# Attention and fp8 feed-forward kernel: the values' products of every head group split over two places, fixed PSUM banks for the side jobs, and four vector and GpSimd steps moved

## The chip, the cores and the metric

The kernel runs on one core of a Trainium2 chip. The metric is the device time of one execution in microseconds (us). Shown are the median of three timed runs and one execution taken by the hardware profiler. The engines are named as in the profile: PE is TensorE, with PEld its weight loads, DVE is VectorE, ACT is ScalarE, POOL is GpSimd, and SP is SyncE, which here issues nearly all DMAs.

## The reference, cut to what matters

Input x has 16 batch rows of 512 tokens with 256 features; there are 16 heads of 16.

```
xn   = layernorm(x)
qkv  = xn @ w_qkv.T + b_qkv
att  = softmax(causal(q k^T / 4 + position_bias))      # position_bias from cos/sin tables and a constant
attn = (att @ v) @ w_proj.T + b_proj
ffn  = bf16(fp8(xn / s_in) @ fp8(kernel / s_k) * s_in * s_k) + bias
out  = x + attn + ffn
```

## The kernel before

The program handles one batch row `b` at a time. The rows 1 to 13 are iterations of one loop; rows 0, 14 and 15 are written out. Every engine has its own instruction stream, and semaphores order them.

**Groups, slots and chunks.** A row has four head groups `g` of four heads. TensorE goes through 12 slots `k` per group, so a row is 48 places (g, k). In each slot it makes one bank of transposed scores (keys by queries, for row b and group g, banks `scoreT_a`, `scoreT_b`, `scoreT_c` in turn; line 648, and 651 for the position features of groups 0 and 1) and, two groups ahead, one bank of scores the other way round (`score_a` to `score_c`, line 625). ScalarE turns the first kind into exponentials in `probs` (L1013); VectorE takes row maxima from the second (L1101, "chunk"). Slots 0 to 3 are 512 columns wide, slots 4 to 7 have 384, and slots 8 to 11 hold 256 and 128. With three banks of each kind TensorE can be three slots ahead of ScalarE and VectorE, no more.

**Side jobs.** After the scores of a slot TensorE runs the jobs that the tables at the head of the file put there. They are:

- `PV`: probabilities times values of the group before (L674), 8 matmul rows per key tile j = 0 to 3. It needs `mask` of POOL for its tile. In some groups the first key tile is made at `PV_AT` and the rest at `PV_REST_AT`.
- `MT`: the transposed row maxima of the next group (L610, L611). It waits for `max_hi` of ScalarE (L908, after the exponential of slot 1), and ScalarE then writes `neg_max_T` (L914), which SP sends into the stacks.
- `QK` and `V` (L560): products of the row after, read by ScalarE (`qk_parts`, `v_rows`) and, for QK, by VectorE (L1089).
- `FF`: the feed-forward product in bf16 (L603), read by ScalarE into `Y1` (L1036; it shares memory with `xnT_bf`).
- `PJ`: the projection of the row before (L560), read by VectorE in `result` (L1114), which stands behind the chunk of slot 1 in group 3.
- `T`: transposes of the normalised input of the row after the next (L568).

All side jobs write to two PSUM banks, `misc_a` and `misc_b`. Each job waits until the reader of the job before it in the same bank is done (function `misc`, table `done`). The kernel before gives the banks in turn along the order of the jobs.

**The other engines around the change.** VectorE also takes statistics for the row after the next (`stats`, L1068), inverts the softmax denominators (`invert`, L1108), and makes three steps of the fp8 quantiser, `quant_magic` (L1125 of 1024 elements, then two of L1130 with two inputs from SBUF). POOL masks (L1324), quantises, computes 1/std (`rstd`, L1291 to L1297), multiplies the attention output by the inverse denominators (`divide`, L1358), splits it (`attn_parts`, L1363), and adds the biases and the feed-forward result. ScalarE rounds the divided attention in `attn_hi` (L992), which `attn_parts` waits for. SP stores the inverses to a scratch tensor in HBM and spreads them back (`store_recips` L411, `spread_recips` L423) into the memory of `XN`, from which `divide` reads.

A job at (g, k) is done by all engines at their own place (g, k); the tables with `_AT` hold these places.

## Time and profile before

| | us |
|---|---|
| median of three runs | 767.23 (766.87 to 767.3) |
| the profiled execution | 769.2 |
| its span, first to last instruction | 767.2 |

The span is 2.0 us short of the profiled execution's time, and close to the median of the others. Granted TensorE clock over the span: 0.99.

| engine | busy, us | share of the span |
|---|---|---|
| PE | 738.7 | 96% |
| DVE | 634.6 | 83% |
| ACT | 586.1 | 76% |
| POOL | 532.4 | 69% |

The end of a matmul is modelled, so the PE share says little on how closely TensorE is packed. What counts is at which time the next instruction starts and what released it. The iterations of the loop are alike within a few hundredths of a microsecond, so one of them stands for all; the rows below are from the iteration of row 6, which covers the time from about 309 to 354 us. In times such as "(2,0)" the first number is the group and the second the slot.

### The profile page before, as it was taken

Reading aid. Unit: us, or ns where it says so; the run is one execution under the profiler, and the core shown is the slowest. Engines: PE = TensorE matmul, PEld = TensorE weight load, DVE = VectorE, ACT = ScalarE, POOL = GpSimd, SP = SyncE. Lnnn points to the kernel's source line nnn. Section 1 sums busy time; section 2 is a strip of 40 time slices with the busy share of each in tenths; the row PEclk is TensorE's granted clock in tenths of the full one; section 3 lists DMA queues with packets and bytes.
Section 4 is the critical chain, followed back from the end, with each engine's and each line's share of the span. In section 5 each row is a group of like instructions: output and inputs, shape, how many; then the busy total and the mean of one; then the engine's idle time right before and its main releaser. Section 6 shows DMA issues by size and latency. Waiting matters only on the chain.

```text
span 767.2 us, 23128 instructions
## 1 busy us (share of the span) xinstructions
PE 738.7 (96%) x6285; PEld 475.1 (62%) x6285; DVE 634.6 (83%) x2401; ACT 586.1 (76%) x1263; POOL 532.4 (69%) x525
## 2 busy tenths in 40 slices
PE   7989999999999999999999999999999999999987
PEld 4656556666765666566566656666665666666555
DVE  4898798889989888988988898898988889888613
ACT  4557888787888878788887878878787888877662
POOL 7445767786777778776777868677776867767571
PEclk9999999999999999999999999999999999999889
DMA  5442353435335433533544253244425334443201
GB/s 181 150 152 103 128 176 142 139 118 178 117 138 174 153 127 118 184 128 121 174 153 141 112 187 136 108 170 152 158 95 193 133 120 153 160 148 108 88 32 62
DMA packets 55313, 105.65 MB, mean 138 GB/s; under 512 B 10421, under 2 KB 30389, under 8 KB 55285
## 3 DMA queue, kind: packets, MB, share of 16 engines
q1 hardware_dynamic: 53968, 104.52, 38.3%
q10 hardware_dynamic: 1316, 0.80, 0.4%
q8 instruction: 13, 0.21, 0.1%
q14 instruction: 16, 0.12, 0.1%
HBM read 18.42 MB, written 8.90 MB: 36 GB/s over the span
## 4 chain that ended last, share of the span: by engine, by line
PE 68%; ACT 11%; DVE 8%; issue 6%; DMA 2%; SPq 2%; DVEq 1%; ACTq 1%; POOLq 0%; POOL 0%
PE misc_a L560 13%; PE misc_a L674 10%; PE misc_b L560 9%; PE scoreT_b L648 9%; PE scoreT_a L648 5%; PE score_c L625 4%; PE misc_b L674 3%; ACT probs L1013 3%; PE score_a L625 2%; PE scoreT_b L651 2%; ACT qk_parts L901 2%; ACT attn_hi L992 2%; DVE row_max L1101 2%; SPq L351 1%; ACT out_T L986 1%
## 5 line engine op out<-in xcount | busy, mean ns | idle before, releaser
L1324 POOL TENSOR_SCALAR_AFFINE_SELECT probs<-probs 128x512 f32<-128x512 f32 x256 | 161.1, 640 | 185.7 <-ACT probs L1013 184.0
L1101 DVE CUSTOM_DVE_ANT_0 score_b<-score_b,causal_mask_q 128x384 f32<-128x384 f32 (+3 forms) x321 | 162.7, 523 | 80.6 <-PE score_b L625 80.3
L1101 DVE CUSTOM_DVE_ANT_0 score_a<-score_a,causal_mask_q 128x512 f32<-128x512 f32 x319 | 174.6, 563 | 2.9 <-PE score_a L625 2.8
L1101 DVE CUSTOM_DVE_ANT_0 score_c<-score_c,causal_mask_q 128x256 f32<-128x256 f32 (+3 forms) x384 | 172.0, 475 | 0.1
L1013 ACT ACTIVATE probs<-scoreT_b 128x384 f32<-128x384 f32 (+1 forms) x256 | 131.8, 515 | 44.7 <-PE scoreT_b L651 21.2
L1013 ACT ACTIVATE probs<-scoreT_a 128x512 f32<-128x512 f32 (+1 forms) x256 | 142.6, 557 | 9.3 <-PE scoreT_a L651 8.0
L1101 DVE DVE_READ_ACCUMULATOR2_ANT row_max<- 128x1 f32 x1024 | 142.8, 139 | 0.0
L1013 ACT ACTIVATE probs<-scoreT_c 128x384 f32<-128x384 f32 (+1 forms) x256 | 133.3, 521 | 1.5 <-PE scoreT_a L648 0.9
L674 PE MATMUL misc_a<-probs,v_ones 128*32 128x128 f32 (+3 forms) x1536 | 124.1, 441 | 3.5 <-DVE xnT_lo L1083 1.3
L648 PE MATMUL scoreT_b<-stacks 64*128 64x384 f32 (+3 forms) x320 | 120.6, 396 | 1.6 <-ACT probs L1013 1.5
L625 PE MATMUL score_b<-stacks 64*128 64x384 f32 (+3 forms) x321 | 116.0, 394 | 0.0
L648 PE MATMUL scoreT_a<-stacks 64*128 64x512 f32 (+3 forms) x320 | 106.6, 353 | 5.5 <-issue 2.1
L625 PE MATMUL score_a<-stacks 64*128 64x512 f32 x319 | 107.9, 370 | 0.3
L648 PEld LDWEIGHTS scoreT_b<-stacks 64*128 64x128 f32 x320 | 56.6, 184 | 77.4 <-ACT probs L1013 45.1
L648 PE MATMUL scoreT_c<-stacks 64*128 64x256 f32 (+3 forms) x384 | 102.4, 299 | 0.3 <-ACT probs L1013 0.3
L625 PE MATMUL score_c<-stacks 64*128 64x256 f32 (+3 forms) x384 | 94.5, 299 | 0.9 <-DVE row_max L1101 0.8
L674 PEld LDWEIGHTS misc_a<-probs,v_ones 128*32 128x32 f32 x1536 | 40.2, 109 | 54.0 <-issue 32.8
L648 PEld LDWEIGHTS scoreT_c<-stacks 64*128 64x128 f32 x384 | 68.6, 186 | 1.2 <-ACT probs L1013 0.9
L625 PEld LDWEIGHTS score_c<-stacks 64*128 64x128 f32 x384 | 65.5, 186 | 5.7 <-DVE row_max L1101 4.4
L625 PEld LDWEIGHTS score_a<-stacks 64*128 64x128 f32 x319 | 54.5, 186 | 15.6 <-DVE row_max L1101 11.1
L648 PEld LDWEIGHTS scoreT_a<-stacks 64*128 64x128 f32 x320 | 57.2, 186 | 11.2 <-issue 5.0
L625 PEld LDWEIGHTS score_b<-stacks 64*128 64x128 f32 x321 | 54.2, 184 | 1.4 <-DVE row_max L1101 1.1
(238 smaller groups left out, 1937.4 us busy)
## 6 DMA issues: line engine op xcount, KB each, us to landing
stacks<-qk_parts SPq DMA_DIRECT2D x128, 512.0 KB, 3.7
x_ring<-in_L_attn_x SPq DMA_DIRECT2D x16, 512.0 KB, 3.6
attn<-out_T SPq DMA_DIRECT2D x63, 128.0 KB, 2.6
xn<-recips SPq DMA_DIRECT2D x31, 256.0 KB
out<-x_ring SPq DMA_DIRECT2D x15, 512.0 KB, 3.0
stacks<-neg_max_T SPq DMA_DIRECT2D x128, 4.0 KB
low_features<-neg_max_T SPq DMA_DIRECT2D x126, 4.0 KB
low_features<-probs SPq DMA_DIRECT2D x8, 128.0 KB, 4.3
```

The lines of the kernel that those rows point to most:

```text
L351: eng.dma_start(max_rows(g, h), MTS[2 * TT * h:2 * TT * h + 2 * TT, g % 2, :].bitcast(F32)) \
L560: last = mm(o, l(ct), r(ct), start=(ct == 0 and i == 0), stop=(ct == CT - 1 and i == 2))
L625: last = mm(SB_[n % 3][:, o:o + w], STK[rows, u, 0, P * qt:P * qt + P], STK[rows, u, 1, 0:w], start=True, stop=True)
L648: last = mm(bank, STK[rows, u, 1, P * j:P * j + P], STK[rows, u, 0, P * j:T], start=True, stop=(g >= 2))
L651: last = mm(bank, EXT[rows, u, 1, P * j:P * j + P], EXT[rows, u, 0, P * j:T], start=False, stop=True)
L674: last = mm(bank[32 * i:32 * i + 32, P * j:T], VA[:, j, HU * g + i, :, :].rearrange("p d a -> p (d a)"), probs(g, j)[:, i, :], start=(j == ...
L901: A(qk_part(m, 0), misc_of("QK", m)[:, :].unsqueeze(1).broadcast_to([P, 2, T]), ACT.Identity, bias=BQ[:, bias:bias + 1]).then_inc(qh_ready, 1)
L986: A(OT[:, :], misc_of("PV", g)[:, :], ACT.Copy).then_inc(ot_ready, 1)
L992: A(AH[:, ct, :], attn_row(b)[:, ct, :], ACT.Copy).then_inc(ah_ready, 1)
L1013: A(probs_slot(g, k), STB[(SLOTS * g + k) % 3][:, 0:w], ACT.Exp).then_inc(exp_done, 1)
L1101: last = V.tensor_tensor_reduce(bank, bank, CMQ[:, T - w:T], 1.0, LEAST, ALU.add, ALU.max, MX[:, g % 2, 8 * h + 4 + qt:8 * h + 5 + qt])
L1324: last = GP.affine_select(out=d, in_=d, compare_op=ALU.is_ge, fill=0.0, base=0, pattern=[[0, HU], [1, P]], channel_multiplier=-1)
```

## The change

Six edits, mostly in the tables:

- `PV` is split in all four groups: the first key tile after slot 0, the rest after slot 3. Before, groups 1 and 2 (whose products are made in the groups 2 and 3 of slots) were made whole after slot 3.
- `FF` is split: one half at (2,0) behind the first tile of PV, one half at (2,6) ahead of the first V job. Its reads on ScalarE move with it.
- The banks are a fixed table: PV in bank a, MT, FF and PJ in bank b, the others in turn.
- VectorE: `invert` moves from (0,8) to (1,3), two of four `stats` from (1,3) to (0,6), and the second `quant_magic` step from (2,2) to (2,3). Its exponents are held in the memory of `VS` instead of `XN`, so that the waits for them sit elsewhere.
- POOL: `divide` comes after the third mask of group 1 instead of before it. ScalarE: both `attn_hi` at (2,4) instead of (2,2) and (2,3).
- SP: the load of x comes before the regroup of the row before, the store of the inverses behind the first stack load, and the spread behind the sends of the maxima of group 2.

The core of the diff:

```diff
-PV_AT = [(1, 0), (2, 3), (3, 3), (0, 0)]
-PV_REST_AT = {0: (1, 3), 3: (0, 3)}
+PV_AT = [(1, 0), (2, 0), (3, 0), (0, 0)]
+PV_REST_AT = [(1, 3), (2, 3), (3, 3), (0, 3)]
-FF_AT = [(2, 0), (2, 0)]
+FF_AT = [(2, 0), (2, 6)]
-AH_AT = [(2, 2), (2, 3)]
-FF_OUT_AT = [(2, 0), (2, 1)]
+AH_AT = [(2, 4), (2, 4)]
+FF_OUT_AT = [(2, 0), (2, 6)]
-INVERT_AT, LAST_INVERT_AT = (0, 8), (2, 11)
+INVERT_AT, LAST_INVERT_AT = (1, 3), (2, 11)
-STATS_AT, AGGR_AT = [(1, 3), (1, 3), (1, 6), (1, 6)], (1, 7)
-MAGIC_AT, FIRST_MAGIC_AT = [(2, 1), (2, 2), (2, 3)], [(0, 1), (0, 3), (0, 4)]
+STATS_AT, AGGR_AT = [(0, 6), (0, 6), (1, 6), (1, 6)], (1, 7)
+MAGIC_AT, FIRST_MAGIC_AT = [(2, 1), (2, 3), (2, 3)], [(0, 1), (0, 3), (0, 4)]
-MISC_BANK = {job: n % 2 for n, job in enumerate(ORDER)}
+MISC_BANK = {(kind, i): bank for kind, banks in (("PV", (0, 0, 0, 0)), ("MT", (1, 1, 1, 1)), ("QK", (0, 1, 0, 1)), ("FF", (1, 1)),
+                                                 ("V", (0, 1)), ("PJ", (1, 1)), ("T", (0, 1))) for i, bank in enumerate(banks)}
...
-        QE = XN[:, :, :].rearrange("p t c -> p (t c)").rearrange("p (a n) -> p a n", n=T)
+        QE = VS[:, :, :].rearrange("p t c -> p (t c)").rearrange("p (a n) -> p a n", n=T)
...
@@ sync, body @@
                 load_stack(b, 3)
-                if not first:
-                    regroup(b - 1, 3, False)
-                load_max(b, 1)
                 if load:
                     ...
                     load_x(b + 2)
                 if not first:
-                    store_recips(b - 1)
+                    regroup(b - 1, 3, False)
+                load_max(b, 1)
...
                     load_stack(b + 1, 0)
                 if not first:
+                    store_recips(b - 1)
+                load_max(b, 2)
+                if not first:
                     spread_recips(b - 1, last)
-                load_max(b, 2)
                 regroup(b, 0, first)
...
@@ scalar @@
                 if i == 0 and not (isinstance(b, int) and b == 0):
                     act.wait_ge(va_ready, b)
+                    act.wait_ge(qm_done, 2 * (b + 1))
...
@@ gpsimd, body @@
                     mask(b, g, 1)
                     if g == 2:
                         ffn_bias(b)
+                    mask(b, g, 2)
                     if g == 1 and not first:
                         divide(b - 1)
-                    mask(b, g, 2)
```

How the instructions stand now. Names with `REGISTER_ALU` or `ISA` and no tile are address and wait bookkeeping.

TensorE at (2,0) to (2,3) in the loop, before: the two FF jobs stand in both banks at slot 0, and the whole of PV behind slot 3.

```order
L603 MATMUL misc_a<-ffn_w_q,xq 128x256 [waits qk_lo_written]
L603 MATMUL misc_a<-ffn_w_q,xq 128x256 x3
L551 REGISTER_ALU
L603 MATMUL misc_b<-ffn_w_q,xq 128x256 [waits qk_lo_written]
L603 MATMUL misc_b<-ffn_w_q,xq 128x256 x3
L648 MATMUL scoreT_b<-stacks 128x512 [waits exp_done]
```

The same place now:

```order
L674 MATMUL misc_a<-probs,v_ones 32x512 [waits probs_masked]
L674 MATMUL misc_a<-probs,v_ones 32x512 x3
L551 REGISTER_ALU [waits ffn_weights_quantised,xq_ready]
L603 MATMUL misc_b<-ffn_w_q,xq 128x256 [waits qk_lo_written]
L603 MATMUL misc_b<-ffn_w_q,xq 128x256 x3
L648 MATMUL scoreT_b<-stacks 128x512 [waits exp_done]
```

One FF half has left the place for (2,6), and the first key tile of PV has come ahead of the other.

TensorE at (3,3) in the loop, before: the first key tile of PV stands between the scores of slot 3 and the MT job, which waits for VectorE's `result` (`out_written`).

```order
L625 MATMUL score_a<-stacks 128x512 [waits chunk_max_done]
L551 REGISTER_ALU
L672 REGISTER_ALU [waits v_rows_written]
L674 MATMUL misc_b<-probs,v_ones 32x512 [waits probs_masked]
L674 MATMUL misc_b<-probs,v_ones 32x512 x3
L608 ISA
L610 MATMUL misc_a<-ident_f32,row_max 32x128 [waits out_written,max_hi_written]
L611 MATMUL misc_a<-neg_ident,row_max_hi 32x128
```

The same place now:

```order
L625 MATMUL score_a<-stacks 128x512 [waits chunk_max_done]
L608 ISA
L610 MATMUL misc_b<-ident_f32,row_max 32x128 [waits out_written,max_hi_written]
L611 MATMUL misc_b<-neg_ident,row_max_hi 32x128
L672 REGISTER_ALU
L674 MATMUL misc_a<-probs,v_ones 32x384 [waits probs_masked]
```

The tile is gone from between them: it now stands at (3,0), ahead of the PJ job that `result` reads. MT still waits for the same two semaphores.

POOL at the end of group 1 in the loop, before:

```order
L1324 AFFINE_SELECT probs<-probs 128x4x128 [waits exp_done,identity_steps]
L357 ISA
L1358 ISA [waits out_T0_regrouped,out_T1_regrouped,inverses_spread,identity_steps]
L1358 TENSOR_TENSOR attn<-attn,xn 128x1024
L357 REGISTER_ALU
L1324 AFFINE_SELECT probs<-probs 128x4x128 [waits exp_done,identity_steps]
L1324 AFFINE_SELECT probs<-probs 128x4x128
```

And now:

```order
L1324 AFFINE_SELECT probs<-probs 128x4x128 [waits exp_done,identity_steps]
L1324 AFFINE_SELECT probs<-probs 128x4x128
L357 ISA
L1358 ISA [waits out_T0_regrouped,out_T1_regrouped,inverses_spread,identity_steps]
L1358 TENSOR_TENSOR attn<-attn,xn 128x1024
```

The division now follows the masks that wait for the last exponential of group 1, and stands directly ahead of `rstd`.

## Rows read from the trace of the kernel before

**Rows 1.** One line of SP (store of the result, its bookkeeping): first and last start.

```profile
L480 SPq FUSED_REGOPS  x13: 110/112/118, 129.5 to 663.0; - x13
```

**Rows 2.** Timeline of PE, (2,0) to (2,4): start, duration, line, output<-inputs, count.

```profile
331.54 0.61 PE L603 MATMUL misc_a<-ffn_w_q,xq 128*128 128x256 bf16 x4
332.35 0.61 PE L603 MATMUL misc_b<-ffn_w_q,xq 128*128 128x256 bf16 x4 [0.20 <-DVE qk_parts L1089]
332.89 0.50 PE L648 MATMUL scoreT_b<-stacks 64*128 64x512 f32 x1
...
334.07 1.06 PE L674 MATMUL misc_a<-probs,v_ones 128*32 128x512 f32 x8
335.07 0.28 PE L610 MATMUL misc_b<-ident_f,row_max 128*32 128x128 f32 x1
...
336.77 0.44 PE L648 MATMUL scoreT_b<-stacks 64*128 64x384 f32 x1
```

**Rows 3.** Timeline of PE, V job at (2,9) to the scores of (3,4).

```profile
340.09 0.38 PE L560 MATMUL misc_b<-w_qkvT_hi,xnT_hi 128*128 128x256 f32 x1
...
344.16 0.50 PE L648 MATMUL scoreT_b<-stacks 64*128 64x512 f32 x1
...
345.06 1.06 PE L674 MATMUL misc_b<-probs,v_ones 128*32 128x512 f32 x8
346.29 0.27 PE L610 MATMUL misc_a<-ident_f,row_max 128*32 128x128 f32 x1 [0.16 <-DVE x_ring L1114]
...
347.98 0.44 PE L648 MATMUL scoreT_b<-stacks 64*128 64x384 f32 x1
```

**Rows 4.** Timeline of DVE: (2,1) to (2,4), and `result` in group 3.

```profile
333.57 0.70 DVE L1101 CUSTOM_DVE_ANT_0 score_b<-score_b,causal_mask_q 128x512 f32<-128x512 f32 x1
...
334.19 0.69 DVE L1125 TENSOR_SCALAR xn<-quant_work 128x1024 int32<-128x1024 int32 x1
...
336.62 0.95 DVE L1130 SCALAR_TENSOR_TENSOR quant_work<-xn,quant_work 128x512 f32<-128x512 f32 x1
337.49 0.55 DVE L1101 CUSTOM_DVE_ANT_0 score_b<-score_b,causal_mask_q 128x384 f32<-128x384 f32 x1
...
345.46 0.69 DVE L1114 TENSOR_TENSOR x_ring<-misc_a,x_ring 128x512 f32 x1
```

**Rows 5.** Timeline of ACT behind the two FF jobs at (2,0).

```profile
332.58 0.71 ACT L1036 ACTIVATE xnT_bf<-misc_a,ffn_scales 128x512 bf16<-128x512 f32 x1
333.43 0.60 ACT L1013 ACTIVATE probs<-scoreT_b 128x512 f32<-128x512 f32 x1
```

**Rows 6.** Timeline of POOL: the division, and a mask of group 2.

```profile
330.33 2.37 POOL L1358 TENSOR_TENSOR attn<-attn,xn 128x1024 f32 x1 [0.51 <-DMA xn<-recips]
...
336.38 0.64 POOL L1324 TENSOR_SCALAR_AFFINE_SELECT probs<-probs 128x512 f32<-128x512 f32 x1
```

**Rows 7.** Three lines over the whole run: durations in ns as min/median/max.

```profile
L1130 DVE SCALAR_TENSOR_TENSOR quant_work<-xn,quant_work x30: 681/690/1021, 69.2 to 692.1; 128x512 f32<-128x512 f32 x30
...
L1363 POOL TENSOR_TENSOR attn_lo<-attn,attn_hi x15: 2352/2818/2824, 114.6 to 734.8; 128x1024 fp32r<-128x1024 f32 x15
...
L1293 POOL TENSOR_TENSOR rstd<-var_eps,neg_half x16: 1022/1023/1557, 9.0 to 645.1; 128x4 f32<-128x4 f32 x16
```

**Rows 8.** Timeline of DVE: the inversion at (0,8), two `stats` at (1,3).

```profile
318.82 0.55 DVE L1108 RECIPROCAL denominators_inv<-denominators 128x64 f32<-128x64 f32 x1
...
324.34 0.74 DVE L1068 BATCH_NORM_STATS2 bn_six<-x_ring 128x6 f32 x2
```

**Rows 9.** Timeline of SP: sends of group 2's maxima; the last row's spread, nothing queued ahead.

```profile
324.93 2.71 SPq L351 DMA_DIRECT2D stacks<-neg_max_T  x4
...
718.93 1.32 SPq L423 DMA_DIRECT2D xn<-recips  x2
```

**Rows 10.** DMA view, 717 to 725 us: busy tenths in 40 slices of 0.2 us.

```profile
DMA  0000004300000000542345455554555322100000
```

**Rows 11.** Page, DMA issues: KB and median us to landing.

```profile
x_ring<-in_L_attn_x SPq DMA_DIRECT2D x16, 512.0 KB, 3.6
```

More of the change, by code:

```diff
@@ L818, in body @@
                                 job_QK(b + 1, i)
+                        for i in due(FF_AT, g, k):
+                            job_FF(b, i)
+                        if not last:
                             for i in due(V_AT, g, k):
                                 job_V(b + 1, i)
-                        for i in due(FF_AT, g, k):
-                            job_FF(b, i)
                         if not first:
@@ L1015, in body @@
                             max_T(b, 1)
+                        for i in due(FF_OUT_AT, g, k):
+                            act.wait_ge(ff_ready, 2 * b + i + 1)
+                            if i == 0 and not last:
+                                act.wait_ge(qz_done, b + 2)
+                            A(Y1[:, 2 * i:2 * i + 2, :], misc_of("FF", i)[:, :].rearrange("p (t c) -> p t c", c=C),
+                              ACT.Identity, scale=SC[:, 3:4]).then_inc(y1_ready, 1)
                         if not last:
@@ L1031, in body @@
                                 attn_hi(b - 1, ct)
-                        for i in due(FF_OUT_AT, g, k):
-                            act.wait_ge(ff_ready, 2 * b + i + 1)
-                            if i == 0 and not last:
-                                act.wait_ge(qz_done, b + 2)
-                            A(Y1[:, 2 * i:2 * i + 2, :], misc_of("FF", i)[:, :].rearrange("p (t c) -> p t c", c=C),
-                              ACT.Identity, scale=SC[:, 3:4]).then_inc(y1_ready, 1)
             body(0, True, False, True)
```

24 lines of the change are left out of this document (10 added, 14 removed).

## The prediction, made before the changed kernel ran

> **What bounds the kernel now.** I read the start times of one row of the batch on TensorE first, then what VectorE, ScalarE and POOL do at the places where TensorE stands still. The loop repeats every 44.46 us: the bookkeeping of one SP line starts 13 times from 129.5 to 663.0, which makes 533.5 / 12 [rows 1]. The shares of busy time do not settle which engine bounds. What matters is that TensorE can be only three slots ahead of ScalarE and VectorE, so the row is a chain of rounds: three slots of scores, then a side job, during which the other two engines eat the three banks. A job that is too long leaves them dry, and a job that waits stops everybody. The two places that the change is about are the start of group 2 [rows 2] and the start of group 3 [rows 3]. In the first, the second FF half starts at 332.35 although the first began at 331.54, released by VectorE; two halves that need 0.54 each (332.35 to 332.89) take 1.35, so about 0.3 is lost. In the second, MT at 346.29 was released by VectorE's `result`, which began at 345.46 and took 0.69 [rows 3, 4]. TensorE lost little there (345.06 plus one tile of PV is 346.06, so 0.23), because the first tile of PV ran meanwhile.
>
> **PV at the start of group 3: about +1.0 per row.** One tile of PV costs 335.07 - 334.07 = 1.00 [rows 2]. Before, from the end of PJ (scores of slot 1 at 344.16) it was 0.90 to the place of the job (345.06), then 1.00 of PV, 0.23 of waiting, and MT at 344.16 + 2.13 = 346.29 [rows 3]. The 2.13 is made by VectorE, not by TensorE: it first needs the chunk of slot 1, then `result` until 346.15 [rows 4], and the change moves neither. Now the tile stands ahead of PJ, so PJ ends 1.00 later, and MT, in bank b like PJ, still waits for the same `result`. It comes 2.13 behind PJ's end again, with nothing left to cover 1.23 of this. From MT to the scores of slot 4 it was 1.69 (346.29 to 347.98), and it is the same work now. So the scores of (3,4) come 1.00 later, counted from the same start of the group. I find nothing behind it that would give this back: from there to the next row ScalarE's work follows the read of PV, which moves too.
>
> **PV and FF in group 2: about +0.1.** Now at (2,0) stand one tile of PV (1.00) and one FF half (0.54): 331.54 + 1.54 = 333.08 against 332.89 [rows 2]. The wait for VectorE is gone, since the tile covers it. Slot 3 is then through at about 334.1 or 334.2, and MT is next. MT needs ScalarE's `max_hi`. ScalarE can read the FF half only from its end, 331.54 + 1.00 + 0.61 = 333.15. Its read takes 0.71, and the exponential of slot 1, which started at 333.43 before [rows 5], now starts at about 333.8; `max_hi` is one exponential later (0.5) and MT starts at about 334.6. This is a new wait of 0.45. MT and the rest of PV take 336.77 - 335.07 = 1.70 [rows 2], so slot 4 starts at 336.3, 0.45 earlier than before. The other FF half (0.54) has gone to (2,6), in front of V, and takes this back: the V job at (2,9) starts at 340.2 where it was at 340.09 [rows 3]. That is +0.1.
>
> **Inversion and statistics: about -0.2.** The inversion takes 0.55 [rows 8] at a place where VectorE runs without a gap, and TensorE waits for a chunk behind it. Moved to (1,3) it takes the place of two `stats`, whose time VectorE had there anyway. The gain is 0.47 at most (0.55 less an overlap of 0.08 with its neighbour), nothing at least, and I take 0.2, since ScalarE is close behind. The `stats` at (0,6) need x earlier. The store of the result is issued at the end of the row before; the load of x now follows as soon as it has landed, and takes 3.6 [rows 11]. By my estimate x is there about 1.3 us before VectorE gets to (0,6). I take nothing.
>
> **Division against the quantiser: +0.3, and the least certain term.** In the rows, VectorE's second step of `quant_magic` (two inputs from SBUF) takes 690 ns as a rule and up to 1021 [rows 7]. The long one shown starts at 336.62 while POOL's mask runs from 336.38 to 337.02 [rows 4, 6], and its follower starts at 337.49, 0.47 after the mask's end. POOL's `attn_parts` behind it has a median of 2818 against a minimum of 2352, and the 4-element power of `rstd` 1557 at most against 1023 [rows 7]. So these steps and POOL's operations shut each other out. The change puts the division, 2.37 of POOL [rows 6], right there. When can it start? The inversion now stands where the two `stats` started, at 324.34, and ends at about 324.9 [rows 8]. SP then has the store (0.4), four sends of maxima (2.71 [rows 9]) and the spread, which it issues at about 328.4. With nothing ahead of it a spread issued at 718.93 keeps the DMA queue busy to slice 35, about 724.0 [rows 9, 10]. That is 5.1, and about 1.3 more pass until POOL starts, estimated from the division at 330.33, which a spread released [rows 6]. So the division starts at 334.4 to 334.8, and the two masks ahead of it (0.64 each) are through before. The first step of `quant_magic` is due at 333.57 + 0.18 + 0.62 = 334.37 [rows 4]. It is nearly a tie. I take the first step as first. Then the division waits for it and ends at about 337.4; the second step, due at 336.2, waits until then, and the chunk of slot 4 starts at 338.5 against 337.49 [rows 4]. VectorE's lateness reaches TensorE through the slots 7 to 9 and costs the V job at (2,9) 0.3 more. If the division is first, the exponent step waits to 336.7, everything on VectorE is 2.1 late, and the V job loses about 1.4 instead of 0.3. If they do not collide at all, it is 0.
>
> The Trainium skill, page "SBUF — State Buffer", section "Who interferes with whom", says that a VectorE instruction with two SBUF inputs, or in a two-port mode, and a GpSimd one share a port pair as an exclusive lock: whichever starts first holds it, the other "fully blocks". The rows agree (690 against 1021 ns). By that rule the loser waits for the whole division, which is what the two cases above do; if the engines shared the bandwidth in proportion instead, I would have put this term at half its size.
>
> **POOL's queue.** The division moves POOL's work behind it by up to 4 us from the place where it stood. POOL then has `rstd`, `attn_parts`, two sorts of masks and `ffn_bias` before PV in group 3 needs the last mask of group 2. Summed up from the division's end at 337.4 it is there at about 346.4, and PV needs it at about 348.4. It is hidden; the reserve is 2 us.
>
> **The sum.** Per row: 1.00 + 0.10 - 0.20 + 0.30 = +1.20. It counts for the rows 1 to 14; row 0 has no PJ and no division, and row 15 no MT at (3,3), and I take nothing for them (at most 0.5 each way). 14 x 1.20 = 16.8. On the profiled execution, 769.2 for a span of 767.2, this gives 786.0. The median of the runs is 2.0 lower, 767.2, so the median of the changed kernel should be **784.0**.
>
> **The rivals.**
> - *The division is first.* For it speaks the tie, and that both times shift together. Per row 1.00 + 0.10 - 0.20 + 1.40 = 2.30, 32 in all: 799.
> - *No collision.* The spread lands much later or earlier, or VectorE's delay is swallowed by its idle time at (2,7). 0.90 per row: 780.
> - *The splitting wins.* This one ends on the other side. The long jobs at (2,3) and (3,3) leave VectorE dry, and each now ends one tile sooner behind its slots. If `result` were through before TensorE comes to MT, slot 4 would come 1.00 earlier after PJ and the tile ahead of PJ would be paid by that; with the saved 0.3 of FF, the 0.23 of MT and the 0.2 of the inversion it is -0.7 per row, so 757. It decides at one point: whether MT in group 3 waits less than 0.3 for `result`. Against it stands that VectorE does `result` only behind the chunk of slot 1, which TensorE makes after PJ.
> - *Nothing to see.* The new wait at MT is eaten by slack that I don't see in ScalarE's chain from (3,4) to the next row: within 0.2% of 767.
>
> **How the numbers follow.** Forecast 0.42, the division first 0.22, no collision 0.21, the splitting wins 0.11, nothing to see 0.04. Slower by over 0.2% (about what a measurement of this kernel can tell from no change): 0.85; within 0.2%: 0.04; faster: 0.11. The range of 8 in 10 leaves out the faster cases; from the low end of the case without collision (0.35 less per row, 775) it goes to a little over the case in which the division is first: 774 to 801.
>
> **What would show it.** The period of the loop should be about 45.7. In group 3, MT should start about 2.1 behind the scores of slot 1, released by `result`, with a gap of 1.2 on TensorE ahead. In group 2, MT should wait about 0.4 for `max_hi`, and no FF job for VectorE. The reciprocal should be followed by the store at once. A step of `quant_magic` should last 1.5 us or more, or the division 2.9 or more. The forecast is wrong if the gap ahead of MT in group 3 is under 0.5, or if TensorE waits for a mask of group 2.

## The result, and the profile after

| | median, us | runs, us | ratio to before (95% interval) |
|---|---|---|---|
| kernel before | 767.26 | 766.87 to 768.08 (4) | |
| changed kernel | 790.4 | 786.83 to 794.81 (4) | 1.0303 (1.0247 to 1.0359) |

The change makes the kernel 3% slower. The ratios, here and in the table of experiments, are taken without the chip's slow runs (the two kernels with an early `result` or changed with early maxima have one each), so a ratio need not be the quotient of the two medians beside it. The profiled execution is the fastest of the four, 786.83 us for a span of 785.1; the granted clock is 0.991 against 0.99 before. The four runs lie 8.0 us apart, those of before 1.2 us. That alone says little: in the measurements beside the experiments the kernel before scatters by 1.35 to 5.3 us, and the granted clocks of the four runs of the changed kernel fall as the time grows, 0.991, 0.990, 0.987 and 0.986 for spans of 785.1, 787.2, 790.1 and 792.8. What is new within one execution are the rows of two lengths that follow here.

**The period.** The line of SP that stood at 129.5 to 663.0 [rows 1] now answers so (duration min/median/max in ns, first and last start in us):

```profile
L480 SPq FUSED_REGOPS  x13: 110/112/123, 128.9 to 678.6; - x13
```

That is 549.7 / 12 = 45.81 us a row against 44.46. But the rows are no longer alike. Taken from the first exponential of one row to that of the next, 9 of the 12 rows 2 to 13 take 45.55 to 45.60 us, and rows 2, 7 and 10 take 46.43 to 46.64. I call these the short and the long rows of this kernel.

**TensorE, start of group 3 of row 6** (start and duration in us, line, output<-inputs; in brackets the idle time ahead and what ended it). It answers to [rows 3]:

```profile
347.53 1.07 PE L674 MATMUL misc_a<-probs,v_ones 128*32 128x512 f32 x8
348.52 0.38 PE L560 MATMUL misc_b<-w_projT_hi,attn_hi 128*128 128x256 f32 x1
...
350.13 0.50 PE L648 MATMUL scoreT_b<-stacks 64*128 64x512 f32 x1
...
352.25 0.27 PE L610 MATMUL misc_b<-ident_f,row_max 128*32 128x128 f32 x1 [1.17 <-DVE x_ring L1114]
...
353.94 0.44 PE L648 MATMUL scoreT_b<-stacks 64*128 64x384 f32 x1
```

The tile of PV stands ahead of PJ and delays it by 348.52 - 347.53 = 0.99. MT comes 352.25 - 350.13 = 2.12 behind the scores of slot 1 (2.13 before), released by the same `result`, and TensorE now stands still for 1.17 where it stood 0.16 [rows 3]. From MT to slot 4 it is 1.69 again.

**TensorE, start of group 2 of row 6**, which answers to [rows 2]:

```profile
336.14 1.06 PE L674 MATMUL misc_a<-probs,v_ones 128*32 128x512 f32 x8
337.14 0.61 PE L603 MATMUL misc_b<-ffn_w_q,xq 128*128 128x256 bf16 x4
337.68 0.50 PE L648 MATMUL scoreT_b<-stacks 64*128 64x512 f32 x1
...
339.29 0.28 PE L610 MATMUL misc_b<-ident_f,row_max 128*32 128x128 f32 x1 [0.54 <-ACT row_max_hi L910]
```

The FF job waits for nobody now, and MT waits 0.54 for `max_hi` instead.

**VectorE and POOL, a short row** (row 6), which answers to [rows 4, 6]:

```profile
338.98 0.69 DVE L1125 TENSOR_SCALAR v_rows<-quant_work 128x1024 int32<-128x1024 int32 x1
...
340.84 2.23 DVE L1130 SCALAR_TENSOR_TENSOR quant_work<-v_rows,quant_work 128x512 f32<-128x512 f32 x2
342.99 0.56 DVE L1101 CUSTOM_DVE_ANT_0 score_b<-score_b,causal_mask_q 128x384 f32<-128x384 f32 x1
```

```profile
339.29 2.62 POOL L1358 TENSOR_TENSOR attn<-attn,xn 128x1024 f32 x1 [1.12 <-issue]
```

The quantiser's first step started at 338.98, and the division, at 339.29, was 0.3 too late to hold it up. The division takes 2.62 instead of 2.37. The next two steps, merged into one line, take 2.23 where two steps without company take 1.29 (below): the first of them takes 1.62 of it and waits for the division's end at 341.91.

**The same places in a long row** (row 7):

```profile
384.55 2.58 DVE L1125 TENSOR_SCALAR v_rows<-quant_work 128x1024 int32<-128x1024 int32 x1
387.06 0.69 DVE L1101 CUSTOM_DVE_ANT_0 score_c<-score_c,causal_mask_q 128x512 f32<-128x512 f32 x1
...
388.31 1.30 DVE L1130 SCALAR_TENSOR_TENSOR quant_work<-v_rows,quant_work 128x512 f32<-128x512 f32 x2
```

```profile
384.22 2.37 POOL L1358 TENSOR_TENSOR attn<-attn,xn 128x1024 f32 x1 [0.45 <-issue]
```

Here the division is first, by 0.33 us. It runs undisturbed to 386.59, and the quantiser's first step lasts 2.58, to 387.13. So a row has one of two outcomes, and which one is a matter of 0.3 us.

**What decides it.** Counted from the exponential of (2,0), the inversion starts at -7.82 to -7.87 in the rows 2 to 13, the spread is issued at -3.87 to -3.92, and the quantiser's first step starts at 2.27 to 2.30. The division starts anywhere from 1.86 to 2.83. So the engines and SP's issue agree within 0.05 us from row to row, and the 1 us of scatter arises between the issue of the spread, a transfer from HBM to SBUF in two issues of 256 KB, and the start on POOL: 5.8 to 6.7 us. POOL stands idle for the last 0.4 to 1.4 us of this. In the DMA records of the trace the last packets of 2 KB of this stretch end 5.1 to 5.9 after the issue, and the division starts 0.6 to 0.8 behind them, so it is the transfer that scatters. Row 6 and row 7 on SP:

```profile
332.80 1.31 SPq L423 DMA_DIRECT2D xn<-recips  x2
...
378.36 1.31 SPq L423 DMA_DIRECT2D xn<-recips  x2
```

Against the division at 339.29 and 384.22 that is 6.5 and 5.9.

### The profile page after: what moved, and what is told of

Same layout as the page of the kernel before. It is cut to its first block, busy times and chain, and to the rows that moved or that the text cites. A ratio compares the mean times of both kernels' runs of the same rounds, so it can differ in the third digit from the quotient of the medians.

```text
span 785.1 us, 23116 instructions
## 1 busy us (share of the span) xinstructions
PE 734.2 (94%) x6285; PEld 476.4 (61%) x6285; DVE 649.3 (83%) x2401; ACT 584.7 (74%) x1263; POOL 532.5 (68%) x525
## 4 chain that ended last, share of the span: by engine, by line
PE 81%; DVE 5%; ACT 5%; issue 5%; DMA 1%; SPq 1%; POOL 1%; DVEq 1%; POOLq 0%; ACTq 0%
PE misc_a L674 19%; PE misc_b L560 16%; PE scoreT_b L648 11%; PE misc_a L560 9%; PE scoreT_a L648 5%; PE score_c L625 5%; PE score_a L625 3%; PE scoreT_b L651 3%; PE misc_b L603 2%; PE misc_b L610 2%; PE scoreT_a L651 2%; PE scoreT_c L651 1%; ACT probs L1013 1%; DVE xnT_lo L1083 1%; ACT xnT_hi L893 1%
## 5 line engine op out<-in xcount | busy, mean ns | idle before, releaser
L1101 DVE CUSTOM_DVE_ANT_0 score_a<-score_a,causal_mask_q 128x512 f32<-128x512 f32 x319 | 176.7, 570 | 3.7 <-PE score_a L625 3.6
L674 PE MATMUL misc_a<-probs,v_ones 128*32 128x512 f32 (+3 forms) x2048 | 165.6, 441 | 3.6 <-DVE xnT_lo L1083 1.2
L1101 DVE DVE_READ_ACCUMULATOR2_ANT row_max<- 128x1 f32 x1024 | 145.2, 142 | 0.0
L648 PE MATMUL scoreT_c<-stacks 64*128 64x256 f32 (+3 forms) x384 | 104.9, 303 | 2.4 <-ACT probs L1013 2.4
L674 PEld LDWEIGHTS misc_a<-probs,v_ones 128*32 128x32 f32 x2048 | 53.5, 109 | 70.8 <-issue 45.8
L986 ACT ACTIVATE out_T<-misc_a 128x512 f32<-128x512 f32 x64 | 38.4, 600 | 47.2 <-PE misc_a L674 47.0
```

The lines of the kernel that those rows point to most:

```text
L648: last = mm(bank, STK[rows, u, 1, P * j:P * j + P], STK[rows, u, 0, P * j:T], start=True, stop=(g >= 2))
L674: last = mm(bank[32 * i:32 * i + 32, P * j:T], VA[:, j, HU * g + i, :, :].rearrange("p d a -> p (d a)"), probs(g, j)[:, i, :], start=(j == ...
L986: A(OT[:, :], misc_of("PV", g)[:, :], ACT.Copy).then_inc(ot_ready, 1)
L1101: last = V.tensor_tensor_reduce(bank, bank, CMQ[:, T - w:T], 1.0, LEAST, ALU.add, ALU.max, MX[:, g % 2, 8 * h + 4 + qt:8 * h + 5 + qt])
```

## The experiments

No kernel leaves out or changes a part of the computation. "Rows" are periods of rows 2 to 13 from first exponential to first exponential. A slot's time is from its exponential to the next. The times of the kernel before were taken beside the kernel in the same line, on the same chip; the chips of different lines can differ. Where a table or function is not in the diff it is the changed kernel's, or, for "the kernel before with", that of the kernel before.

| kernel | median (runs), us | before, us | ratio (95% interval) |
|---|---|---|---|
| PV of group 2 in its old place | 778.86 (776.14 to 780.27) | 768.28 | 1.0143 (1.0108 to 1.0178) |
| TensorE's part alone | 794.73 (790.39 to 798.19) | 768.28 | 1.0359 (1.0316 to 1.0401) |
| the other part alone | 775.3 (773.26 to 777.12) | 768.28 | 1.0099 (1.0063 to 1.0134) |
| quantiser's first step at (2,2) | 793.57 (792.16 to 799.02) | 768.28 | 1.0352 (1.0302 to 1.0402) |
| quantiser's first step at (2,0) | 782.2 (780.53 to 783.73) | 767.37 | 1.0176 (1.0148 to 1.0204) |
| TensorE's part, result first | 790.27 (779.82 to 793.42) | 767.37 | 1.0215 (1.0137 to 1.0294) |
| before, maxima early | 765.95 (762.69 to 768.71) | 767.37 | 0.9974 (0.9955 to 0.9993) |
| changed, maxima early | 788.0 (784.02 to 799.28) | 767.37 | 1.0245 (1.0192 to 1.0298) |
| result first, low part later | 768.42 (763.97 to 771.3) | 768.0 | 0.9994 (0.9972 to 1.0016) |
| division's places back | 889.73 (885.46 to 891.11) | 768.0 | 1.1557 (1.1519 to 1.1594) |
| the other part without collision | 777.8 (774.96 to 778.03) | 768.0 | 1.012 (1.0098 to 1.0142) |
| division's and statistics' places back | 780.35 (778.02 to 781.3) | 767.06 | 1.0175 (1.0158 to 1.0192) |

**1. Is the PV tile ahead of PJ the whole 1.0 us?** Only this is undone:

```diff
-PV_AT = [(1, 0), (2, 0), (3, 0), (0, 0)]
-PV_REST_AT = [(1, 3), (2, 3), (3, 3), (0, 3)]
+PV_AT = [(1, 0), (2, 0), (3, 3), (0, 0)]
+PV_REST_AT = {0: (1, 3), 1: (2, 3), 3: (0, 3)}
```

> The changed kernel with one thing undone: in group 3 the first key tile of PV stands again behind slot 3, ahead of MT, and no longer ahead of PJ. Theory (the tile covered the wait for result): MT starts 2.1 behind the scores of slot 1 as before, but with a gap of 0.2 instead of 1.2 ahead of it, so 1.00 less per row in rows 1 to 14: loop period 44.56 where it is 45.56, and 14 us less than the changed kernel, 773 to 781. Rival (the fixed banks make the loss, or the tile's place does not matter): no change, 786 to 795.

Measured 778.86, 11.5 below the changed kernel, in the expected range, where the theory said 14. The slot (3,0) falls from 2.69 back to 1.69, the value of before. The banks stay fixed in this kernel, so they are not what costs the 1.00. TensorE around MT of group 3, row 5:

```profile
300.82 0.50 PE L648 MATMUL scoreT_b<-stacks 64*128 64x512 f32 x1
...
301.72 1.07 PE L674 MATMUL misc_a<-probs,v_ones 128*32 128x512 f32 x8
302.94 0.27 PE L610 MATMUL misc_b<-ident_f,row_max 128*32 128x128 f32 x1 [0.16 <-DVE x_ring L1114]
...
304.63 0.44 PE L648 MATMUL scoreT_b<-stacks 64*128 64x384 f32 x1
```

MT is 2.12 behind slot 1 here too. So `result` paces this place, and the tile is all but free behind slot 3 and costs its full length ahead of PJ. The division still meets the quantiser: 8 short rows of 44.57 to 44.75, and 4 of 45.26 to 45.75.

**2. The two halves of the change, each alone.** TensorE's part is `PV_AT`, `PV_REST_AT`, `FF_AT`, `FF_OUT_AT` and the bank table put into the kernel before; the other part is the changed kernel with these taken back.

> The kernel before with only the TensorE part of the change: PV split everywhere, FF split, fixed banks. Division, inversion, quantiser, statistics and the SP order stay as before. Theory: +1.00 in group 3 and +0.1 in group 2 per row, period 45.56, 782 to 783, and the runs agree within 0.5 us, since the division stays away from the quantiser. Rival (splitting wins by itself and the other part costs it): 757 to 767.

> The changed kernel with the TensorE part taken back: only division, inversion, statistics, quantiser, attn_hi and the SP order are as in the change. Theory: -0.2 per row from the inversion and +0.3 (division second) to +1.3 (division first) from the collision: 769 to 783, with runs that differ by several us from each other. Rival (this part is harmless alone): 764 to 767 and runs within 0.5 us.

The other part came out as expected, 775.3, with 11 rows of 44.48 to 44.85 and one of 45.78. TensorE's part did not: 794.73 instead of 782 to 783, no faster than both parts together (1.0359 against 1.0303, with intervals that overlap), and its runs are 7.8 apart where I had expected 0.5. Its rows are of 45.4 to 45.6 (7 of 12), as expected, or of 47.0 to 47.2 (5 of 12). VectorE and POOL in a long row (row 3) and in a short one (row 4):

```profile
205.17 0.69 DVE L1103 CUSTOM_DVE_ANT_0 score_a<-score_a,causal_mask_q 128x512 f32<-128x512 f32 x1
205.77 2.92 DVE L1132 SCALAR_TENSOR_TENSOR quant_work<-xn,quant_work 128x512 f32<-128x512 f32 x1
...
252.83 0.69 DVE L1132 SCALAR_TENSOR_TENSOR quant_work<-xn,quant_work 128x512 f32<-128x512 f32 x1
```

```profile
205.76 2.39 POOL L1365 TENSOR_TENSOR attn_lo<-attn,attn_hi 128x1024 fp32r<-128x1024 f32 x1
...
252.84 2.93 POOL L1365 TENSOR_TENSOR attn_lo<-attn,attn_hi 128x1024 fp32r<-128x1024 f32 x1
```

(L1132 and L1365 are L1130 and L1363 of the kernel before.) It is the same contention with another partner: the third step of the quantiser against the subtraction of the low part. The starts differ by 0.01 us, one way or the other, and the loser takes 2.92 instead of 0.69, or 2.93 instead of 2.39. At less than 0.01 us the recorded starts no longer tell the winner: in row 1 of experiment 1 the division is recorded 8 ns ahead of the quantiser's first step and yet is the one that waits (2.94 against 0.69). In the kernel before the subtraction starts 0.32 to 0.46 behind that step in each of these rows, so that tie never arises; TensorE's part removes that gap. Whether the loser is VectorE or POOL makes 1.7 us a row. The changed kernel escapes this, since its `AH_AT` of (2,4) puts the subtraction later, and gets the tie with the division in exchange.

**3. The quantiser's first step shifted by one slot, each way.** The one entry of `MAGIC_AT` that meets the division:

```diff
-MAGIC_AT, FIRST_MAGIC_AT = [(2, 1), (2, 3), (2, 3)], ...
+MAGIC_AT, FIRST_MAGIC_AT = [(2, 2), (2, 3), (2, 3)], ...
```

> The changed kernel with the first step of quant_magic one slot later, at (2,2). It is then due about 0.6 us later, so that the division has always started before it. Theory: every row of 1 to 14 is like the slow ones of the changed kernel, period 46.6, 795 to 798, and the runs agree within 1 us. Rival (the long rows come from something else, such as a late DMA landing): the same 787 to 795 and the same difference between runs.

```diff
-MAGIC_AT, FIRST_MAGIC_AT = [(2, 1), (2, 3), (2, 3)], ...
+MAGIC_AT, FIRST_MAGIC_AT = [(2, 0), (2, 3), (2, 3)], ...
```

> The changed kernel with the first step of quant_magic one slot earlier, at (2,0), so that it is always through before the division starts. Theory: every row is like the fast ones of the changed kernel, period 45.56, 782 to 784, and the runs agree within 1 us. Rival (the long rows come from something else): the same 787 to 795 and the same difference between runs.

L1125 over the whole run, in ns as min/median/max: the changed kernel, then the step later, then earlier:

```profile
L1125 DVE TENSOR_SCALAR v_rows<-quant_work x16: 689/690/2636, 45.1 to 705.1; 128x1024 int32<-128x1024 int32 x16
```

```profile
L1125 DVE TENSOR_SCALAR v_rows<-quant_work x16: 689/2059/2811, 44.6 to 710.0; 128x1024 int32<-128x1024 int32 x16
```

```profile
L1125 DVE TENSOR_SCALAR v_rows<-quant_work x16: 689/694/726, 45.0 to 699.2; 128x1024 int32<-128x1024 int32 x16
```

One slot earlier the first step never loses, and the time is 782.2, as expected. But the rows are not all alike: they take 45.2 to 46.1, and the runs lie 3.2 apart instead of under 1. The second step, due 3.9 after the exponential of (2,0), now meets the division in every row and lasts 1.15 to 2.43, the longer the later the division starts. One slot later the first step loses in 11 of the 12 rows, which take 45.7 to 46.8, and the time is 793.57. The two times bracket the changed kernel's 790.4. The later kernel came out 1.4 below the expected 795, and its runs scatter by 7 instead of under 1: I had taken a lost start as one fixed price, but the wait lasts until the division ends, and the division's start varies (L1125 of 1.8 to 2.8 us).

**4. The changed kernel without any collision.** First the division, the reciprocals, the inversion and SP's order went back to their old places:

```diff
-INVERT_AT, LAST_INVERT_AT = (1, 3), (2, 11)
+INVERT_AT, LAST_INVERT_AT = (0, 8), (2, 11)
...
+                if not first:
+                    regroup(b - 1, 3, False)
+                load_max(b, 1)
                 if load:
                     ...
                     load_x(b + 2)
                 if not first:
-                    regroup(b - 1, 3, False)
-                load_max(b, 1)
+                    store_recips(b - 1)
...
-                    mask(b, g, 2)
                     if g == 1 and not first:
                         divide(b - 1)
+                    mask(b, g, 2)
```

> The changed kernel with the reciprocals and the division where they were before (SP's order, POOL's order and INVERT_AT), all else as changed. Theory: the division starts about 2 us before group 2 again and meets no step of the quantiser, so no row is left to a start that is first by chance: rows of 45.3 to 45.6 us (before's 44.46, +1.0 at (3, 0), nothing or little in group 2, no gain from the inversion), time 779 to 783, runs within 1.5 us of each other. Rival: the scatter and the rest of the loss come of the new buffer of the exponents or of the other places; then the time stays at 786 or more and runs differ by 4 us or more.

Missed: it took 889.73, over 7 us a row more than any other kernel here. The undoing was not clean. VectorE in row 4:

```profile
255.91 0.60 DVE L1101 CUSTOM_DVE_ANT_0 score_a<-score_a,causal_mask_q 128x384 f32<-128x384 f32 x1
263.38 0.75 DVE L1068 BATCH_NORM_STATS2 bn_six<-x_ring 128x6 f32 x2 [6.81 <-DMA x_ring<-in_L_attn_x]
```

The statistics, still at (0,6), wait 6.8 us for an x that SP now issues only at 259.77, behind four sends of maxima. Groups 2 and 3 of this kernel behaved as the theory says (the steps at 0.69), but its time is worthless for the question. With the statistics back too:

```diff
-STATS_AT, AGGR_AT = [(0, 6), (0, 6), (1, 6), (1, 6)], (1, 7)
+STATS_AT, AGGR_AT = [(1, 3), (1, 3), (1, 6), (1, 6)], (1, 7)
```

> The changed kernel with the division, the reciprocals, the inversion and SP's order where they were before, and now the statistics of x at (1, 3) too, so that VectorE does not wait at (0, 6) for an input that SP loads later (7.2 us a row in the run before this one). Theory: no step of the quantiser meets a long POOL operation, rows of 45.3 to 45.5 us (before's 44.46, 1.0 of it at (3, 0), group 2 within 0.1 of before), time 779 to 783, runs within 2 us of each other: the 8 to 10 us that the changed kernel takes above this are the collision's. Rival: the loss and the scatter above 783 come of another of the new places (attn_hi as a pair at (2, 4), the exponents' buffer); then the time is 786 or more and the runs differ by 4 us or more.

Measured 780.35, all rows 45.39 to 45.55, runs 3.3 apart. Row 4 on VectorE and POOL, and the quantiser's L1130 over the run:

```profile
246.68 0.69 DVE L1125 TENSOR_SCALAR v_rows<-quant_work 128x1024 int32<-128x1024 int32 x1
...
248.54 1.29 DVE L1130 SCALAR_TENSOR_TENSOR quant_work<-v_rows,quant_work 128x512 f32<-128x512 f32 x2
```

```profile
242.60 2.37 POOL L1358 TENSOR_TENSOR attn<-attn,xn 128x1024 f32 x1 [0.59 <-DMA xn<-recips]
```

```profile
L1130 DVE SCALAR_TENSOR_TENSOR quant_work<-v_rows,quant_work x32: 680/685/690, 47.0 to 703.2; 128x512 f32<-128x512 f32 x32
```

The longest of 32 steps is 690 ns, where it was 2318 in the changed kernel. So 13.3 of the 23.1 us stay with TensorE's places and those of `attn_hi` and the quantiser, and 10 go with the new places of the division, the reciprocals, the inversion and the statistics.

Not all of these 10 are contention. The two profiled executions, with spans of 785.1 and 776.0, differ by 6.0 in the rows 2 to 14, in which neither trace has a stretch below full clock: 4.4 in the rows 2 to 13 and 1.6 in row 14. That is the collision, less the inversion's gain of 0.2 a row. Another 3.0 lie behind the first exponential of row 15, where the granted clock is 0.50 for 13.4 us in the changed kernel and for 6.2 here. That is TensorE's clock in this one execution (0.996 over the span), and it fits experiment 5, where 3.4 us at half clock cost 1.4. The other three runs of this kernel have 0.990 to 0.992 and spans of 778.2 to 779.6.

**5. Could the splitting win, if `result` were early?** That was the rival that ended on the other side. In this kernel (TensorE's part alone) PJ is made ahead of the PV tile, `result` stands ahead of the chunk of slot 1, and the maxima are rounded one slot earlier:

```diff
-MAX_AT, FIRST_MAX_AT = 2, (0, 1)
+MAX_AT, FIRST_MAX_AT = 1, (0, 1)
-RESULT_AT = [(3, 1), (3, 6)]
+RESULT_AT = [(3, 0), (3, 6)]
+                        if not first:
+                            for i in due(PJ_AT, g, k):
+                                job_PJ(b - 1, i)
                         if not (first and g == 0):
                             ...
                             if (g, k) == PV_AT[pg]:
```

> The kernel before with the TensorE part of the change, and three more moves that take away what MT waits for: PJ ahead of the tile of PV at (3,0), result of VectorE at (3,0) instead of (3,1), and max_hi of ScalarE ahead of the exponential of slot 1. Theory (the loss is the wait of MT and nothing else): no gap ahead of MT in groups 2 and 3; -0.2 in group 3 and -0.3 in group 2 against the kernel before, 758 to 764. Rival (splitting PV costs by itself, by the second drain or by starving the others): 770 to 783.

Missed: 790.27. But MT in group 3 waits for nobody (a short row, 6):

```profile
357.56 1.06 PE L675 MATMUL misc_a<-probs,v_ones 128*32 128x512 f32 x8
358.56 0.49 PE L649 MATMUL scoreT_b<-stacks 64*128 64x512 f32 x1
...
359.46 0.28 PE L611 MATMUL misc_b<-ident_f,row_max 128*32 128x128 f32 x1
...
361.16 0.44 PE L649 MATMUL scoreT_b<-stacks 64*128 64x384 f32 x1
```

and the short rows take 44.37 to 44.64, 1.0 less than with TensorE's part alone. The other 6 of 12 rows take 47.54 to 47.64, each with a third step of 2.90 to 2.93: the tie of experiment 2. A long row loses 3.1 here and 1.7 in TensorE's part alone, for the same 2.9 us step, and the granted clock tells why. Shown are row 2 of this kernel behind the lost tie, then row 3 of TensorE's part alone, as start:end, length, busy time and count of PE, PEld, DVE, ACT and POOL, granted clock, DMA share and GB/s:

```profile
163.00:165.00 2.00, 1.56 (x10) 1.16 (x11) 2.00 (x9) 1.09 (x4) 1.37 (x2) 1.00 0.20 72
165.20:168.60 3.40, 3.40 (x22) 3.14 (x20) 1.30 (x9) 1.24 (x4) 1.16 (x1) 0.50 0.00 0
```

```profile
211.00:215.00 4.00, 4.00 (x36) 2.79 (x35) 3.06 (x18) 2.09 (x5) 2.30 (x3) 1.00 0.19 71
```

Each of the 6 long rows here has one stretch of 3.4 us at 0.50, which is 1.2 GHz, and none of the short ones has; in TensorE's part alone no row has one. The stretch costs the difference, 1.4 us. Between the tie and the fall of the clock TensorE's longest wait is 0.60 us. Why much the same waits leave the clock alone in the other kernel is open.

If the tie is all, moving the subtraction must remove the long rows:

```diff
-AH_AT = [(2, 2), (2, 3)]
+AH_AT = [(2, 4), (2, 4)]
```

> The kernel with the result's evacuation first (TensorE's part alone, PJ ahead of the PV tile, RESULT_AT (3, 0), MAX_AT 1), and beside it only the change's AH_AT, both evacuations of attn_hi at (2, 4). Theory: the rows of 47.6 us of that kernel are those in which the subtraction of the low part on POOL (2.4 us) starts just before the quantiser's third step, 0.00 to 0.02 us apart; with attn_hi at (2, 4) the subtraction starts after that step in every row. All rows then take 44.3 to 44.6 us, the time is 764 to 768, and runs agree within 1.5 us. Rival: the slow rows come of TensorE's order in group 2 (the second FF job in front of a V job); then rows of 47 stay, the time stays 779 to 793 and the runs differ by several us.

All rows now take 44.41 to 44.72, no row from 2 to 13 has a stretch below full clock, and the time is 768.42, against 768.0 of the kernel before (0.9994, 0.9972 to 1.0016). The runs did not come within the expected 1.5 us of each other: the ten lie 7.3 apart, with granted clocks from 0.996 for the fastest to 0.985 for the slowest. The third step over the run, L1132 with its longest at 946 ns against 2931:

```profile
L1132 DVE SCALAR_TENSOR_TENSOR quant_work<-xn,quant_work x30: 680/686/946, 68.3 to 692.5; 128x512 f32<-128x512 f32 x30
L1365 POOL TENSOR_TENSOR attn_lo<-attn,attn_hi x15: 2349/2390/2402, 114.7 to 736.5; 128x1024 fp32r<-128x1024 f32 x15
```

So one line of a table was worth 22 us, the clock lost behind the tie included. The split order, given an early `result`, comes out even with the old one, not faster: slot (3,3) falls from 2.33 to 1.70 and (3,6) from 1.01 to 0.86, but (3,0) stays at 2.68 against 1.69. And this kernel also rounds the maxima early, which alone gives the kernel before 0.9974 (experiment 6); against that, the split order is 0.2% behind, with intervals that overlap.

**6. Rounding the maxima earlier, by itself.** It removes the 0.54 wait of MT ahead of group 2's slot 4, if that wait is on the path. One entry, in the kernel before and in the changed one:

```diff
-MAX_AT, FIRST_MAX_AT = 2, (0, 1)
+MAX_AT, FIRST_MAX_AT = 1, (0, 1)
```

> The kernel before with max_hi of ScalarE ahead of the exponential of slot 1. Theory: MT in the kernel before is covered by the tile of PV and waits for result in group 3 only, so there is next to nothing to gain: 765.5 to 767.5. Rival (max_hi is what makes MT late everywhere): -0.4 per row, 760.

> The changed kernel with max_hi of ScalarE ahead of the exponential of slot 1. Theory: the gap ahead of MT in group 2 goes (0.45), of which VectorE's lateness takes back most; the gap in group 3 stays, since it waits for result: -0.1 to -0.4 per row, 782 to 790. Rival (max_hi is the cause in group 3 too): the gap in group 3 goes as well, -1.2 per row more, under 775.

Before with it: 765.95 over 10 runs, 0.9974 (0.9955 to 0.9993), rows 44.36 to 44.43. This is the fastest version found, by a quarter of a per cent. Changed with it: 788.0, ten rows of 45.35 to 45.72, and two of 46.70 and 48.16, both with the division first. The rows with the quantiser first are 0.2 shorter than in the changed kernel, the gap ahead of MT in group 3 stays at 1.17. The longer of the two, row 9, is the only row of this kernel's rows 2 to 13 with a stretch at half clock, which again costs 1.4 to 1.5 us for 3.4:

```profile
478.10:481.50 3.40, 3.40 (x22) 3.18 (x20) 1.87 (x8) 1.57 (x4) 2.90 (x2) 0.50 0.11 41
```

**7. The gain of the inversion without the collision.** The other part alone, with the maxima early and the quantiser around the division instead of in it:

```diff
-MAGIC_AT, FIRST_MAGIC_AT = [(2, 1), (2, 3), (2, 3)], ...
+MAGIC_AT, FIRST_MAGIC_AT = [(2, 0), (2, 5), (2, 5)], ...
```

> The changed kernel without TensorE's part, with MAX_AT 1, and the quantiser's first step at (2, 0), the other two at (2, 5). Theory: the division runs between 2.1 and 5.4 us of group 2, the first step is over before it and the two others start behind it, so the inversion's 0.2 us a row stays as a gain, and MAX_AT's 0.07: rows of 44.2 to 44.3 us, time 761.5 to 764, faster than the kernel before by 0.4 to 0.7%. Rival: two steps of 0.69 us at (2, 5), where VectorE prepares a slot every 0.37, delay the slots from (2, 6) on and the V evacuation that waits for them by as much as the collision did: rows of 44.5 to 45.2, time 766 to 776.

The theory missed, and the time lies where the rival put it, a little above its range: 777.8, rows 44.64 to 44.72 with two of 45.1. The rows account for 3.5 of the 9.8 us over the kernel before; the rest lies outside the rows 2 to 13 and in the clock (0.985 to 0.987), and I have not divided it up. No step collides with the division; in the two rows of 45.1 the third step meets the subtraction of the low part (1.12 instead of 0.69). (1,0) takes 1.25 instead of 1.45. Group 2 gives back more. In the table of slots, (2,3) takes 2.57 instead of 1.93, (2,4) 1.41 instead of 0.37 behind both `attn_hi`, and (2,9) 1.89 instead of 1.64; (2,2) and (2,6) save 0.52 and 0.71 of it. By this, VectorE has no hole there that two steps of together 1.29 us fit into, and the next chunk begins only behind them:

```profile
249.75 0.60 DVE L1099 CUSTOM_DVE_ANT_0 score_c<-score_c,causal_mask_q 128x384 f32<-128x384 f32 x1
250.26 1.29 DVE L1128 SCALAR_TENSOR_TENSOR quant_work<-v_rows,quant_work 128x512 f32<-128x512 f32 x2
251.47 0.56 DVE L1099 CUSTOM_DVE_ANT_0 score_a<-score_a,causal_mask_q 128x384 f32<-128x384 f32 x1
```

That it is these steps, and not the two `attn_hi` in a row, that cost most is argued from the slots, not shown by a run of its own. For it speaks experiment 5: there the same move of `attn_hi` takes (2,4) from 0.37 to 1.41, and the short rows grow by no more than 0.1, since (2,2) and (2,6) give about 1.0 back.

## Why the prediction came out as it did

Direction and range were right (790.4 in 774 to 801). The point, 784.0, was 6.4 us too low. By its own terms, per row:

| term | predicted | measured | from |
|---|---|---|---|
| PV ahead of PJ | +1.00 | +1.00 | slot (3,0), 1.69 to 2.69; back to 1.69 in experiment 1 |
| behind it, to the next row | 0 | -0.06 | slot (3,6), 1.01 to 0.95 |
| PV and FF in group 2 | +0.10 | +0.04 | slots of group 2 without collision (experiment 4), 10.97 against 10.93 |
| inversion and statistics | -0.20 | -0.20 | slot (1,0), 1.45 to 1.25 |
| collision, quantiser first | +0.30 | +0.35 | (2,9) of 1.53 against 1.18 in experiment 4 |
| collision, division first | +1.40 | +1.2 to +1.4 | long rows, 46.43 to 46.64, against 45.56 less 0.35 |
| a short row in all | +1.20 | +1.10 | 45.56 against 44.46 |
| a long row in all | +2.30 | +2.0 to +2.2 | |

**What was right.** That `result` paces MT, and that a tile moved in front of PJ has nothing to hide behind. That MT in group 2 takes over a wait of about 0.45 (0.54). The spread's way: 5.1 + 1.3 = 6.4 us from issue to the division, against 5.8 to 6.7. The near tie itself: both price tags of the collision hold within 0.1 or 0.2. The small sum of group 2 is right with other parts than I had: (2,4) takes 1.41 instead of 0.37 behind the two `attn_hi`, which I had not priced at all, and (2,1), (2,2) and (2,9) give it back; that the sum holds is luck. The Trainium skill, page "SBUF — State Buffer", section "Who interferes with whom", describes this as an exclusive lock in which whichever starts first holds it; the runs agree, down to the 0.01 us to which the records order two starts: a 0.69 us step lasts 2.92 when the other engine started 0.01 us earlier, and a 2.39 us subtraction lasts 2.93 when it started 0.01 us later.

**What failed** is the step that made one case out of the tie. I took "the first step as first" for all rows and gave the other order to a rival in which the division is first in every row, "and that both times shift together". They do not shift together: the quantiser's start repeats within 0.03 us, and the transfer in front of the division scatters by 1 us, so each row draws anew. In the profiled execution 3 of 12 rows are long, by 1.0, which is 0.25 a row over a short one's 1.10, in all the 1.35 measured. Row 14, written out and not in the loop, lost 2.27 (45.42 against 43.15), where I had counted it as a row of 1.20; without the collision it loses 0.67 (43.82). The sum for the profiled execution was 786.0 and it took 786.83. That it misses by 0.8 only is luck: the rows 1 to 14 grew by 19.4 where I had 16.8, and the time outside them, for which I had nothing, fell by 1.8 (1.1 ahead of the first exponential, 0.5 in row 0). Another 2.0 is the step from the profiled execution to the median, which I took over from the kernel before (769.2 to 767.2) and which did not hold. The last 3.6 is that here the median run lies above the profiled one. Part of it is the clock: the two runs around the median have granted clocks of 0.990 and 0.987. In the profiled run 13.4 us are at half clock, in these, by the same share, some 16 and 21; at 1.4 us lost for 3.4, as in experiment 5, that is about 2 of the 3.6, by my estimate. The rest would be one or two long rows more. The other runs left no traces, so this last step is worked out, not seen. The rows are a mixture of both cases, and the mixture lies above the case that I took.

**The rivals.** "No collision, 780" has nearly the number of experiment 4, 780.35, but not its parts: that kernel has given back the inversion's gain, so by my terms it should have been at 1.10 a row, and its rows 2 to 13 took 0.98. "The division is first, 799" is nearly experiment 3's later step, 793.57, and misses since its wait is mostly shorter than I supposed. "The splitting wins" was decided at the point named: MT waits 1.17, not under 0.3. Experiment 5 shows that even with that wait gone it would have been even, not 757. "Nothing to see" is out at 3%.

## What to carry to other kernels

A long operation with two SBUF inputs on POOL and a short one on VectorE shut each other out for their whole length, and who loses is decided by which starts first, as far as the records can order the starts. A moved step is therefore to be placed by the start times of its neighbours on the other engine, with a margin over the scatter of whatever releases them; where a DMA releases one of them, that scatter is about 1 us here, and a place inside it makes the row a draw. The sign of it is a row time that jumps between two values within one execution; look there for two engines' instructions whose starts differ by less than that scatter. Scatter between whole runs is not that sign by itself: the kernel of experiment 5 without long rows scatters by 7.3 us over ten runs, in step with its granted clock. And a job that was free beside a wait costs its full length once it is moved in front of what the wait is for.

## What the runs showed of the hardware that I had not expected

- A difference of 0.01 us in the starts of two engines costs or saves 1.7 us a row, or 3.1 where the granted clock falls behind it (experiments 2 and 5). Moving one of the two instructions away took a kernel from 790.3 to 768.4.
- A transfer of two times 256 KB, issued at the same point of each row within 0.05 us, releases its reader 5.8 to 6.7 us later.
- A wait of TensorE can cost more than its length. In the kernel of 889.73 TensorE has nothing to do from about 260.1 to 264.7. Its granted clock, in stretches given as start:end, length, busy time and count of PE, PEld, DVE, ACT and POOL, clock, DMA share and GB/s:

```profile
258.00:260.00 2.00, 2.00 (x11) 1.29 (x8) 0.00 (x0) 1.64 (x5) 1.51 (x2) 1.00 0.02 6
260.00:262.00 2.00, 0.10 (x1) 0.00 (x0) 0.00 (x0) 0.94 (x1) 0.00 (x0) 1.00 0.46 148
262.00:264.00 2.00, 0.00 (x0) 0.00 (x0) 0.62 (x2) 0.00 (x0) 0.00 (x0) 0.59 0.33 115
264.00:266.00 2.00, 1.05 (x8) 0.76 (x8) 2.00 (x9) 0.35 (x1) 0.00 (x0) 0.50 0.00 0
...
270.00:274.00 4.00, 4.00 (x37) 1.98 (x35) 2.17 (x6) 2.04 (x5) 2.64 (x3) 0.68 0.80 280
274.00:280.00 6.00, 6.00 (x47) 4.62 (x48) 5.06 (x22) 4.57 (x9) 1.70 (x2) 1.00 0.23 71
```

The clock falls to 0.50 (1.2 of 2.4 GHz) while TensorE is idle and is back at 1.00 only some 8 us after it has work again. VectorE's wait is 6.8 us, TensorE's own is 4.6, and the row is 8.0 longer (53.46 against 45.44 on average). So 1.2 to 3.4 of it is over, and I put it down to the clock; no run separates the two. The waits of 1.2 us in the changed kernel cost no clock: its trace has no stretch below full clock ahead of row 15. Waits of 0.55 to 0.60 us stood ahead of the fall in every long row of experiment 5, so the length of the wait alone does not tell.
